# Attention with ALiBi on one core: two quarters share one block of output rows, and TensorE's order within a quarter changes

## The reference

```python
def attention(x, Wqkv, Wout):          # on the layer-normed x
    q, k, v = split(x @ Wqkv)          # 16 heads of 8 features
    logits = q @ k.T / sqrt(8) + slope[head] * (j - i)
    logits = where(i >= j, logits, -inf)
    return (softmax(logits) @ v) @ Wout
```

## Time and profile before

| | |
|---|---|
| median of three runs | 874.27 us (874.11 to 877.36) |
| the profiled execution, its own time | 877.4 us |
| its span | 875.6 us |
| attention, first to last exponential | 415.3 to 628.2 us |
| busy share of the span | PE 71%, DVE 71%, POOL 52%, ACT 51% |
| granted TensorE clock over the span | 0.865 |

### The profile page before, as it was taken

The page is one execution under the profiler, slowest core; times in us unless marked ns, Lnnn a source line. Parts: engine busy times, 40 slices in busy tenths (PEclk is TensorE's granted clock), DMA queues, the critical chain, the costliest instruction groups (busy, mean ns, idle before and its releaser), DMA issues. The chain is left out here.

```text
span 875.6 us, 21952 instructions
## 1 busy us (share of the span) xinstructions
PE 618.8 (71%) x7826; PEld 454.7 (52%) x7826; DVE 622.3 (71%) x1397; ACT 443.5 (51%) x873; POOL 458.8 (52%) x591
## 2 busy tenths in 40 slices
PE   0569975780089999125899999999714884999950
PEld 0354433560069999113556666655502563999940
DVE  6997887682078888387778888888513872888856
ACT  5634456760045556162767666666603332555534
POOL 1238758887557777410003223565765880677760
PEclk9968987995579999755899999999956996999985
DMA  9510002341044554332123233241110412444518
GB/s 287 144 38 1 0 8 70 71 90 50 32 83 90 94 94 89 132 116 70 57 64 90 67 88 87 80 119 52 42 34 28 83 34 48 85 100 96 100 28 283
DMA packets 131850, 70.51 MB, mean 81 GB/s; under 512 B 89535, under 2 KB 118725, under 8 KB 131746
## 3 DMA queue, kind: packets, MB, share of 16 engines
q1 hardware_dynamic: 121042, 50.46, 23.9%
q0 software_dynamic: 9088, 16.88, 6.8%
q10 hardware_dynamic: 1616, 1.77, 0.7%
HBM read 26.61 MB, written 30.50 MB: 65 GB/s over the span
## 5 line engine op out<-in xcount | busy, mean ns | idle before, releaser
L1500 ACT ACTIVATE ARENA<-banks,ARENA 128x256 f32<-128x256 f32 x312 | 122.3, 476 | 98.7 <-PE banks L1460 94.4
L2226 DVE TENSOR_REDUCE ARENA<-banks 128x4 f32<-128x1024 f32 (+1 forms) x128 | 122.8, 959 | 39.2 <-PE banks L1970 37.7
L1458 PE MATMUL banks<-ARENA,W1H 128*128 128x256 f16 x312 | 88.1, 282 | 62.3 <-DMA ARENA<-slots 61.5
L2148 ACT ACTIVATE ARENA<-banks 128x1536 f32<-128x1536 f32 x64 | 92.7, 1448 | 38.2 <-PE banks L1994 38.2
L1472 PE MATMUL banks<-W2L,ARENA 128*128 x624 | 110.0, 219 | 2.3 <-DVE ARENA L1513 2.3
L1474 PE MATMUL banks<-W2H,ARENA 128*128 x624 | 109.7, 219 | 0.0
L1473 PE MATMUL banks<-W2H,ARENA 128*128 x624 | 109.7, 219 | 0.0
L1448 POOL DMA_INDIRECT expert_out_g<-ARENA x78 | 77.8, 997 | 48.8 <-issue 26.2
L1448 POOL DMA_INDIRECT expert_out_f<-ARENA x78 | 81.4, 1043 | 33.1 <-issue 23.5
L1532 DVE TENSOR_TENSOR ARENA<-ARENA 128x1024 f16<-128x1024 f32 x78 | 95.6, 1225 | 2.7
L1058 POOL DMA_INDIRECT slots<-ARENA,PLACE x64 | 77.4, 1210 | 26.0 <-issue 17.5
(11 more groups left out here) (324 smaller groups left out, 1773.2 us busy)
## 6 DMA issues: line engine op xcount, KB each, us to landing
spread<-ARENA SPq DMA_DIRECT2D x96, 64.0 KB
ARENA<-expert_out_f SPq DMA_DIRECT2D x8, 512.0 KB, 7.6
ARENA<-spread SPq DMA_DIRECT2D x16, 256.0 KB, 3.0
ARENA<-spread SPq DMA_DIRECT2D x32, 128.0 KB, 2.8
ARENA<-expert_out_g SPq DMA_DIRECT2D x8, 512.0 KB, 7.3
XT<-in_w SPq DMA_DIRECT2D x10, 256.0 KB, 7.7
slots<-EMPTY SPq DMA_DIRECT2D x16, 129.0 KB, 4.3
ARENA<-in_w SPq DMA_DIRECT2D x8, 256.0 KB, 6.6
```

The source lines that it names most:

```text
L1458: pe.matmul(out, t.W1H[:, e, ms], XST[i][:, 0], start=True, stop=False)
L1500: ins = nc.scalar.activation(HF[i % 2][:, m], UP[i % 2][:, m], ACT.Gelu, bias=BIAS[i % 4][:, m:m + 1], scale=1.0 / WS)
L2148: nc.scalar.activation(PR[x % 2], t.psum_all[:, 5:8, :], ACT.Exp, scale=1.0 / LOGIT).then_inc(exps, 1)
L2226: dve.tensor_reduce(MX[:, G // 2, tile, :, :, G % 2].rearrange("p s a -> p a s"), src, AX.X, ALU.max).then_inc(m_red, 1)
```

## The change

Two quarters that follow one another (a pair) share the 32 output rows of each of the four blocks: the even quarter's head goes to rows 0 to 15, the odd one's to rows 16 to 31. For the odd quarter the weights of the matmul are a slice that begins 16 columns ahead of its head, so that zeros meet the first 16 rows, and the product is added to what the even quarter left. Bank 4 then holds a pair in 256 columns, `take_out` copies 256 columns for 512, and `turn_back` needs 2 transposes for 4 (64 for 128 over the attention). `normalise` reads the heads at a step of 16. Which head is in which quarter changes, so the projection weights and the ALiBi rows are put in another order on the host. TensorE's order within a quarter becomes: scores, first maxima, weighting, routing matmuls where there are any, second maxima, pieces.

```diff
@@ -1761,7 +1761,7 @@
         KST = [carve(F16, HG, SEQ) for _ in range(3)]
         DENSE = [carve(F16, 4, SEQ) for _ in range(2)]
         PR = [carve(F32, 3, BANK) for _ in range(2)]
-        OT = [carve(F32, HG, SEQ) for _ in range(2)]
+        OT = [carve(F32, 2, SEQ) for _ in range(2)]
         ATT = carve(F32, TPB, D)
         ATH, ATL = carve(F16, SEQ), carve(F16, SEQ)
         MX = carve(F32, 2, TPB, 2, 2, 2)
@@ -2019,13 +2019,15 @@
                     pe.wait_ge(vset, c + 1)
                 if G % 2 == 0:
                     after(pe, ot_set, 2 * c + G // 2)
-                half = ps[4][:, SEQ * (G % 2):SEQ * (G % 2) + SEQ]
+                pair, odd = divmod(G, 2)
                 for g in range(GH):
-                    out = half[32 * g:32 * g + 32, :]
+                    out = ps[4][32 * g:32 * g + 32, 0:SEQ]
+                    first = 32 * (2 * GH * pair + 2 * g + odd) - 16 * odd
+                    own, other = (V32[c % 2][:, tile].rearrange("p h e -> p (h e)")[:, first:first + 32] for tile in range(TPB))
                     early = PR[G % 2][:, g // 2, SEQ * (g % 2):SEQ * (g % 2) + SEQ]
                     late = PR[G % 2][:, 2, P * g:P * g + P]
-                    pe.matmul(out, V32[c % 2][:, 0, 4 * G + g, :], early, start=True, stop=False)
-                    ins = pe.matmul(out[:, P:2 * P], V32[c % 2][:, 1, 4 * G + g, :], late, start=False, stop=True)
+                    pe.matmul(out, own, early, start=odd == 0, stop=False, skip_group_check=True)
+                    ins = pe.matmul(out[:, P:2 * P], other, late, start=False, stop=odd == 1, skip_group_check=True)
                 ins.then_inc(av_mm, 1)
 
             def turn_back(c, tile):
@@ -2035,8 +2037,8 @@
                     after(pe, added, c)
                 else:
                     pe.wait_ge(att, 2 * c + 1)
-                for G in range(HG):
-                    ins = pe.transpose(ps[1][:, P * G:P * G + P], OT[c % 2][:, G, P * tile:P * tile + P], t.ID)
+                for pair in range(2):
+                    ins = pe.transpose(ps[1][:, P * pair:P * pair + P], OT[c % 2][:, pair, P * tile:P * tile + P], t.ID)
                 ins.then_inc(ft_mm, 1)
 
             def turn_out(c):
@@ -2055,10 +2057,12 @@
 
             def quarter_of(b, G):
                 x = HG * b + G
+                if quarter(x):
+                    scores(x)
                 if quarter(x + 4):
                     maxima(x + 4, 0)
-                if quarter(x):
-                    scores(x)
+                if quarter(x - 1):
+                    weigh(x - 1)
                 if G == 3:
                     if gate_group(b) is not None:
                         for c in range(4 * gate_group(b), 4 * gate_group(b) + 4):
@@ -2098,8 +2102,6 @@
                     middle.turn(pe, 3)
                 if b == 0:
                     middle.turn(pe, 4 + G)
-                if quarter(x - 1):
-                    weigh(x - 1)
                 if G == 1 and batch(b + 1):
                     values(b + 1)
 
@@ -2149,8 +2151,7 @@
 
             def take_out(c, half):
                 act.wait_ge(av_mm, 4 * c + 2 * half + 2)
-                nc.scalar.activation(OT[c % 2][:, 2 * half:2 * half + 2, :], ps[4].rearrange("p (g n) -> p g n", n=SEQ),
-                                     ACT.Copy).then_inc(ot_set, 1)
+                nc.scalar.activation(OT[c % 2][:, half, :], ps[4][:, 0:SEQ], ACT.Copy).then_inc(ot_set, 1)
 
             def out_high(c):
                 act.wait_ge(fa_mm, c + 1)
@@ -2236,7 +2237,7 @@
 
             def normalise(c, tile):
                 dve.wait_ge(ft_mm, 2 * c + tile + 1)
-                src = ps[1].rearrange("p (h d) -> p h d", d=32)
+                src = ps[1][:, 0:2 * P].rearrange("p (h d) -> p h d", d=16)
                 dve.reciprocal(RC[:, tile, :], src[:, :, 8]).then_inc(rc_set, 1)
                 dve.wait_ge(rc_set, 2 * c + tile + 1)
                 tt(ATT[:, tile, :].rearrange("p (h d) -> p h d", d=8), src[:, :, 0:8],
@@ -2383,7 +2384,8 @@
     rows = np.zeros((2, HD, GH, HG, SEQ), np.float16)
     rows[0, 0:2] = WQ
     by_group = (high, (steps - high.astype(np.float64)).astype(np.float16))
-    rows[1, 0], rows[1, 1] = (v.reshape(HG, GH, SEQ).transpose(1, 0, 2) for v in by_group)
+    rows[1, 0], rows[1, 1] = (
+        v.reshape(2, GH, 2, SEQ).transpose(1, 0, 2, 3).reshape(GH, HG, SEQ) for v in by_group)
     rows[1, 3], rows[1, 7] = 1024, 1024
     c["first_row"] = np.tile(np.arange(NE) * float(STRIDE), (P, 1))
     c["slotno"] = np.arange(SLOTS).reshape(1, SLOTS)
@@ -2458,7 +2460,7 @@
     arrays["w2"] = np.concatenate([of("ffn_w2"), of("ffn_ws2")[None]])
     arrays["b1"] = np.concatenate([of("ffn_b1"), of("ffn_bs1")[None]]).reshape(NX, MT, P).transpose(2, 0, 1)
     arrays["b2_rows"] = np.broadcast_to(np.concatenate([of("ffn_b2"), of("ffn_bs2")[None]]), (P, NX, D))
-    arrays["w_qk"] = of("attn_b_Wqkv")[:, 0:2 * D].reshape(D, 2, HG, 2, 2, HD).transpose(0, 1, 4, 3, 5, 2).reshape(D, 2 * D)
+    arrays["w_qk"] = of("attn_b_Wqkv")[:, 0:2 * D].reshape(D, 2, 2, 2, 2, 2, HD).transpose(0, 1, 4, 3, 6, 2, 5).reshape(D, 2 * D)
     arrays["w_vo"] = np.concatenate([of("attn_b_Wqkv")[:, 2 * D:], of("attn_b_Wout")], 1)
     arrays["gate_w"] = of("ffn_gate_w")
     arrays["gate_b"] = np.broadcast_to(of("ffn_gate_b"), (P, NE))
```

## The result

The changed kernel takes 870.13 us (median of five runs, 869.57 to 873.49) against 874.94 of the kernel before in the same comparison (five runs). The ratio is 0.994, 95% interval 0.9923 to 0.9957, so 0.6% or about 5 us faster. A second comparison gave 0.9937 (0.9919 to 0.9956). The forecast was 868.0 us in a range of 861.5 to 874.5, by way of 6.25 us less; the medians of this comparison are 4.8 us apart.

What follows compares the result with a forecast made beforehand. PE and DVE wait for each other by turns in a ring of 3.08 us a quarter. Gains 8.45 + 0.4 - 1.2 - 1.4 = 6.25 us take the profiled 877.4 to 871.1, median 868.0 us; range 861.5 to 874.5.

Steps and rivals of the forecast that it cites:

- The ring: First and second maxima on PE and their DVE reductions share two banks: no quarter shorter than 3.08 us.
- The walk: Step-by-step timing of one batch's four quarters in the new order: 12.77 us in place of 13.42, 0.65 less.
- PE's stall: PE stalls beside the short reduction, 0.31 us, four times a batch 1.24; weighting fills it in the new order.
- PE's wait for R0 falls below 0.15 a quarter: Sign of being right: PE waits under 0.15 us a quarter for the DVE's first, short reduction.
- The transposes count for little: Two fewer PE transposes save 0.29 us in G = 2 and 3; without that, G = 3 first maxima start 10.66, not 10.61.
- Rival 4: The transposes were the bound: all 9.3 us come back, 865 us, stall stays 0.31; chance 0.56 with the forecast.
- By itself worth nothing: ACT's 256-column copy, 0.38 for 0.60 us, saves 7 us of ACT; worth nothing alone, but shortens one chain.
- Rival 1: PE's added tile-shape changes, 0.27 us a batch, are paid in full: 871.8 us; chance 0.24 with other small losses.
- Rival 2: Scores heading PE's queue hold first maxima in G = 3: 881.0 us if ACT is 1.5 us late; chance 0.12.
- Fourteen batches count: Batches before POOL's statistics in the 15th gain: the first 0.4 us, thirteen at 0.65 are 8.45.
- That 0.13 is inside the 0.24: G = 0 scores wait 0.13 us for row maxima, inside first maxima's 0.24 us wait for the ring.
- as fixed in length: POOL's work ending the stage, from the statistics at 608.64 to 653.2, keeps its length.

Runs made afterwards that it cites:

- the row maxima first: Changed kernel with SP sending the row maxima of G = 0 and 1 before it stores queries and keys: 868.31 us, ratio 0.9922.
- the packing alone: Changed kernel with PE's old order, keeping 16-row halves, two transposes and 256-column copies: ratio 0.9921 to the kernel before.
- the long copy: Changed kernel with the copy of a pair writing each of its 256 columns twice: ratio 0.9942 to the kernel before.
- the order that makes the ring longer: Changed kernel with PE's order first maxima, scores, weighting, second maxima, pieces: 894.63 us, ratio 1.0218.
- all three moves: Changed kernel with row maxima sent before the store, last four batches' statistics and normalisation earlier, second-half copy before `highs` in G = 0: 865.42 us, ratio 0.9879.

## Why the prediction held, point by point

- **The ring.** Shown. The walk said 12.77 us a batch; it is 12.71 where no transfer is late (12.70 to 12.77 with the row maxima first), and the same sum gave 13.0 to 13.2 for the order alone (13.04), 12.95 to 13.05 for the packing alone (13.04), 12.85 to 12.9 with the transposes back (12.83), 12.95 to 13.0 with the long copy (12.93) and 14.7 for the order that makes the ring longer (14.65). Two of these lie 0.02 below their range.
- **PE's stall.** It goes, but the sign "PE's wait for R0 falls below 0.15 a quarter" is not met in the list it was to be read from: 0.28 stands ahead of second maxima in G = 0 and 2. The 0.31 of the prediction was a mean over first and second maxima; that the real stall was about as long shows in the scores, which take 0.68 us, as reckoned, now that first maxima follow them at once.
- **"The transposes count for little."** True beside the new order, 0.12 a batch where the walk implied about 0.1, although two of them still take 0.36 where 0.30 was taken. By itself the sentence misleads: in the old order the packing, transposes and copy, gives 0.38 a batch, as much as the order. Rival 4, in which the transposes were the bound and PE's stall stays, falls with the changed kernel and is close to the truth for the packing alone, where the wait does stay at 0.32.
- **"By itself worth nothing" for the copy.** Right in its second half: the chain through weighting in G = 1 takes all of the 0.22 a batch.
- **Rival 1, the changes of tile shape.** First maxima to weighting is 502.43 to 502.75, 0.32, so 0.09 above the 0.23 of the matmuls, as reckoned. The Trainium skill, TensorEngine Tiling (Array Packing), Tiling Modes under Key Properties, has a mode switch drain the engine; the trace agrees that a gap stands there. The ring hides it in this quarter: second maxima come 0.75 after the short reduction begins, and not later, and first maxima to the short reduction is 0.46, not above the 0.5 that would have spoken for the rival.
- **Rival 2, the head of PE's queue.** Its mechanism is there, its size is not. In most batches scores wait little; in one batch of each of the two profiled runs of the changed kernel they wait 1.3 us for the row maxima, and once for the exponential that waits for POOL, 2.2 us on ACT in place of 1.8.

The sum, though, came out near in part by luck: four of its terms have to be set right, and their errors largely cancel. (The 863.5 at the lower end of "the forecast alone" is worked out nowhere.)

1. **"Fourteen batches count"** took the way to the twelfth statistics as whole batches. In the new order the short reduction, and with it the statistics behind it on the DVE, stands later in the quarter. The exponential of G = 0 and POOL's statistics of the same quarter, before and after:

```profile
459.07 1.45 ACT L2148 ACTIVATE ARENA<-banks 128x1536 f32<-128x1536 f32 x1 [1.64 <-PE banks L1994]
...
459.56 0.20 POOL L1111 TENSOR_TENSOR NRM<-RSTATS 128x2 f32<-128x2 f32 x1 [38.59 <-DVE RSTATS L2248]
```

```profile
457.68 1.45 ACT L2150 ACTIVATE ARENA<-banks 128x1536 f32<-128x1536 f32 x1 [0.81 <-PE banks L1994]
...
459.22 0.20 POOL L1111 TENSOR_TENSOR NRM<-RSTATS 128x2 f32<-128x2 f32 x1 [38.49 <-DVE RSTATS L2249]
```

0.49 us before, 1.54 after: 1.05 us lost once, which the sum left out. It is why the first statistics come only 0.34 earlier, although the exponential comes 1.39 earlier. Most of it comes back at the end of the stage, in point 4.

2. **"That 0.13 is inside the 0.24"**: the landing of the row maxima was taken from the median of another transfer, 2.8 us. Scores went on 3.39 us after the issue in the first profiled run and 3.46 in the second, and waited 1.3 us each time. In the eighth batch counted from the first statistics (563.32 - 549.41 = 13.91, before 567.49 - 554.12 = 13.37) the wait turned a gain of 0.65 into a loss of 0.54. In the second run a like loss stands in the third batch, 13.91 (before 13.43), and the eighth takes 12.67. The rows of before that answer to the 549.41 and 563.32 above are (POOL's timeline):

```profile
554.12 0.20 POOL L1111 TENSOR_TENSOR NRM<-RSTATS 128x2 f32<-128x2 f32 x1 [5.97 <-DVE RSTATS L2248]
...
567.49 0.19 POOL L1111 TENSOR_TENSOR NRM<-RSTATS 128x2 f32<-128x2 f32 x1 [0.60 <-DVE RSTATS L2248]
```

3. **The three batches that POOL's routing holds**, from 563.32 to 604.08, took 40.76 us after and 608.64 - 567.49 = 41.15 before: 0.4 gained. My terms for them, 3 x 0.65 - 0.6 - 1.4, say about 0; close, and so is 40.74 with the packing alone. The term of 1.4 for ACT's wait is too large by itself: that wait grew by 0.4, from 1.8 to 2.2.

4. **The tail "as fixed in length"** is 1.3 shorter: from the twelfth statistics to the next stage 55.12 before, 53.84 after. POOL waited 0.97 us for ACT's normalisation behind the twelfth statistics:

```profile
614.67 0.40 POOL L1126 CAST ARENA<-XN 128x256 f16<-128x256 f32 x1 [0.97 <-ACT XN L1134]
```

Now it does not wait there (the row at 609.20 above). A shorter batch is not the reason: the order alone and the packing alone have batches of the same length, and from the twelfth statistics to the next it is 11.46 us with the order alone (11.45 with both changes) and 12.37 with the packing alone, as before. So it is the order: the statistics come later in the quarter with G = 0, and so closer to ACT's normalisation in G = 2. That is 0.92 of the 1.28; where the rest comes from was not followed.

The terms against the trace: the first three batches 0.34 + 1.05 = 1.39 (predicted 0.4 + 2 x 0.65 = 1.7), less 1.05 for the later place; seven batches to 549.41, 94.56 - 90.19 = 4.37 (predicted 7 x 0.65 - 0.6 = 3.95); the eighth batch -0.54 (predicted 0.65); three batches 0.39 (predicted -0.05); the tail 1.28 (predicted 0). Together 5.84, against 6.25; by the medians of the result it is 4.8.

Why the packing alone (0.9921) is as fast as both stays open in part. Its profiled run has no wait of scores for the row maxima, which gives it back 0.90 in the eighth batch (13.01 against 13.91), but it keeps the longer end of point 4, 0.90, and loses 1.75 over the seven batches before. From the first exponential to the next stage it takes 1.5 and 0.3 us longer than the two runs of the changed kernel. The intervals of the times overlap, so they do not contradict this. The version with all three moves made the changed kernel faster than either, 0.9879.

## What to carry to other kernels

When two engines pass a buffer back and forth, write down the ring with its four distances before counting work: it tells which work can be hidden, where a block must stand, and what a worse order costs (here 2.2%). When the order of a loop moves, ask two more questions: at what point of the loop its consumers now get their data, and which transfer is now wanted earlier. Before a wait is put down to what stands beside it, look at a second run of the same kernel: here the wait was there again, and its neighbour was not. An engine with 30% idle time can still set the pace where one of its copies stands between two waits.

## What was not expected of the hardware

The first two transfers of row maxima (4 KB each) took 3.39 us from SP's issue at 557.62 until the waiting scores went on at 561.01, beside POOL's indirect DMAs. They took 3.46 (490.48 to 493.94) in the second run with no such DMA beside them, and there scores beside POOL's DMAs went on at 558.48 without a wait, 2.85 after the issue at 555.63. What makes them late is open. Two stages that no kernel here changed differ by up to 2.8 us between profiled runs (209.0 to 211.8 us from the start of the shared expert's stage to the end of the span), which is half of what the change brings, and the attention of the changed kernel began at 415.2 us in one run and 412.6 in the other; a single pair of profiles could not have told the size of this gain.
